# Weights applied in the expert stage: what a routed row carries, and who copies it

## The reference, cut to what matters

```python
xn = _layernorm(x)                        # x: (4, 1024, 256)
s = attention(xn)                         # 16 heads of 16, causal, with decay, then @ o_w.T + o_b
probs = softmax(xn @ gate_w)              # 8 experts
gate_score, gate_idx = top_k(probs, 2)
gate_score = gate_score / sum(gate_score)
combine = einsum('tk,tke->te', gate_score, onehot(gate_idx)) * alpha[None, :]
h = gelu(einsum('th,ehi->eti', xn, fc1_w) + fc1_b[:, None, :])
y = einsum('eti,eih->eth', h, fc2_w) + fc2_b[:, None, :]
g = silu(einsum('eth,te->th', y, combine))
out = x + s * g
```

## Time and profile before

| | us |
|---|---|
| median of 3 runs (703.76 to 708.72) | 706.3 |
| the profiled execution | 707.9 |
| its span, first to last instruction | 706.1 |
| TensorE busy | 681.8 (97%) |
| VectorE busy | 534.2 (76%) |
| ScalarE busy | 483.9 (69%) |
| GpSimd busy | 240.1 (34%) |
| mean granted TensorE clock | 0.980 |

### The profile page before, as it was taken

The page is one execution under the profiler, slowest core; times in us unless marked ns, Lnnn a source line. Parts: engine busy times, 40 slices in busy tenths (PEclk is TensorE's granted clock), DMA queues, the critical chain, the costliest instruction groups (busy, mean ns, idle before and its releaser), DMA issues.

```text
span 706.1 us, 16193 instructions
## 1 busy us (share of the span) xinstructions
PE 681.8 (97%) x5370; PEld 453.1 (64%) x5370; DVE 534.2 (76%) x1146; ACT 483.9 (69%) x994; POOL 240.1 (34%) x336
## 2 busy tenths in 40 slices
PE   7998999999999999999999999999999999999985
PEld 4886676455555556555555555554379999999764
DVE  6566887999999999999999999996234554444298
ACT  3553344577787877788787778878776666666374
POOL 4261211233023433333343332300035857575300
PEclk9999999899999999999999999999999999999998
DMA  6999786123445564555556456510189686855396
GB/s 209 283 302 369 250 268 206 36 76 80 106 150 134 137 184 138 146 158 169 132 141 174 147 135 160 157 41 19 47 191 282 243 227 194 240 177 176 123 396 248
DMA packets 74802, 124.46 MB, mean 176 GB/s; under 512 B 13832, under 2 KB 44296, under 8 KB 74600
## 3 DMA queue, kind: packets, MB, share of 16 engines
q1 hardware_dynamic: 65104, 95.26, 46.6%
q0 software_dynamic: 9616, 28.17, 12.4%
HBM read 72.64 MB, written 49.72 MB: 173 GB/s over the span
## 4 chain that ended last, share of the span: by engine, by line
PE 82%; DVE 9%; DMA 3%; ACT 2%; issue 2%; POOL 0%; SPq 0%; POOLq 0%; DVEq 0%; ACTq 0%
PE ps L1607 20%; PE ps L1591 14%; PE ps L1538 13%; PE ps L1695 9%; PE ps L1717 9%; PE ps L1527 6%; PE ps L1490 5%; DVE mxa L1132 3%; PE ps L1500 3%; PE ps L1678 2%; DMA q_parts<-arena 2%; ACT arena L993 1%; DVE x_room L1445 1%; DVE arena L1440 1%; DVE arena L1430 1%
## 5 line engine op out<-in xcount | busy, mean ns | idle before, releaser
L1132 DVE TENSOR_REDUCE mxa<-ps 128x1 f32<-128x512 f32 (+3 forms) x608 | 358.3, 655 | 34.8 <-PE ps L1527 21.2
L993 ACT ACTIVATE arena<-ps 128x512 f32<-128x512 f32 x576 | 302.8, 605 | 76.1 <-PE ps L1591 38.6
L1591 PE MATMUL ps<-aug 59*128 59x512 f32 (+3 forms) x768 | 216.4, 403 | 0.7 <-ACT arena L993 0.5
L1538 PE MATMUL ps<-aug 57*128 57x512 f32 (+3 forms) x768 | 212.5, 402 | 3.4 <-DVE mxa L1132 1.9
L1591 PEld LDWEIGHTS ps<-aug 59*128 59x128 f32 x768 | 112.5, 188 | 78.9 <-ACT arena L993 69.2
L1607 PE MATMUL ps<-arena,v_q 128*32 128x512 f32 (+3 forms) x1536 | 156.6, 503 | 1.0 <-ACT arena L993 1.0
L1538 PEld LDWEIGHTS ps<-aug 57*128 57x128 f32 x768 | 109.9, 188 | 41.6 <-DVE mxa L1132 25.2
L886 POOL DMA_INDIRECT xs_dram<-arena,slot x64 | 62.8, 981 | 81.9 <-ACT arena L993 78.5
L913 POOL DMA_INDIRECT y_dram<-arena,y_row_of x71 | 69.6, 981 | 47.0 <-DVE y_row_of L1369 38.6
L1527 PE MATMUL ps<-key_mask,key_rows 64*128 64x128 bf16 (+2 forms) x352 | 77.4, 254 | 0.0
L1695 PE MATMUL ps<-arena 128*128 128x128 f32 x568 | 75.2, 275 | 0.0
(11 more groups left out here) (150 smaller groups left out, 642.0 us busy)
## 6 DMA issues: line engine op xcount, KB each, us to landing
aug<-k_parts SPq DMA_DIRECT2D x96, 128.0 KB
aug<-q_parts SPq DMA_DIRECT2D x96, 128.0 KB
arena<-xs_dram SPq DMA_DIRECT2D x71, 128.5 KB
k_parts<-arena SPq DMA_DIRECT2D x16, 512.0 KB, 4.7
q_parts<-arena SPq DMA_DIRECT2D x16, 512.0 KB, 4.5
arena<-y_dram SPq DMA_DIRECT2D x16, 512.0 KB, 7.7
xn_dram<-arena SPq DMA_DIRECT2D x8, 512.0 KB, 5.6
a_dram<-arena SPq DMA_DIRECT2D x128, 32.0 KB
```

The source lines that it names most:

```text
L993: nc.scalar.activation(prob_slot(q, i), score_bank(q, i), ACT.Exp).then_inc(exp_done, 1)
L1132: nc.vector.tensor_reduce(dst, src, AX.X, ALU.max).then_inc(piece_used, 1)
L1538: ins = nc.tensor.matmul(banks[:, at_ * width:(at_ + 1) * width], k_aug[n][rows, hp, ib * P:(ib + 1) * P], q_aug[n][rows, hp, lo:lo + widt ...
L1591: ins = nc.tensor.matmul(out_[:, col0:col0 + hi - lo], q_aug[n][rows, h // SIDES_OF_ARRAY, jb * P:(jb + 1) * P], k_aug[n][rows, h // SIDES ...
```

## The change

A routed row is 258 words: row number, weight, 256 values. `scatter` copies the weight next to the number with a second small copy. In the expert stage `take_row` moves from VectorE to GpSimd and copies both words; three of these copies come ahead of GpSimd's loop, the others inside it, three tiles ahead of the store. VectorE, after the bias, multiplies the tile with its rows' weights in a second instruction; for this it waits for its own addition (`y_biased`) and for `row_taken`. TensorE waits for `y_biased` where it waited for `y_out`. `y_evacuate` takes the expert number from the register that `h_evacuate` read. In the last stage ScalarE's scaling is gone, and VectorE adds the two choices with one instruction for the pair. `row_and_weight` lies in the room of `logits`.

```diff
@@ -12,7 +12,8 @@
 
 P = 128
 B, T, D = 4, 1024, 256
-W = D + 1
+LEAD = 2
+W = D + LEAD
 H, HD = 16, 16
 E = 8
 KT = D // P
@@ -225,16 +226,6 @@
 
 def is_last(q):
     return isinstance(q, int) and q == NQ - 1
-
-
-def in_turn(ahead, what):
-
-    for m in range(AHEAD_OF_PRODUCT):
-        ahead(m)
-    for m in range(NT // 2):
-        what(m)
-        if m + AHEAD_OF_PRODUCT < NT // 2:
-            ahead(m + AHEAD_OF_PRODUCT)
 
 
 def attention_moe_kernel(nc, x, wqT, wkT, wvT, woT, qb, kb, vb, ob, gate, w1, b1, w2, b2, alpha,
@@ -295,14 +286,14 @@
         weight = sb("weight", [P, NT, 2])
         slot = sb("slot", [P, NT, 2], i32)
         tile_expert = sb("tile_expert", [P, SLOTS], i32)
-        y_row_of = sb("y_row_of", [P, SLOTS], i32)
+        row_and_weight = logits[:, :, :].rearrange("p t e -> p (t e)")[:, 0:LEAD * SLOTS].bitcast(i32).rearrange("p (n r) -> p n r", r=LEAD)
         y_row = sb("y_row", [P, NT, 2], i32)
         blank = sb("blank", [P, W])
-        zeros = blank[:, 1:W]
+        zeros = blank[:, LEAD:W]
         pad_slot = sb("pad_slot", [P, E], i32)
         spare_f = sb("spare_f", [P, E, 2])
         spare = sb("spare", [P, E, 2], i32)
-        ARENA = 16 * 1024 + CH
+        ARENA = 16 * 1024 + LEAD * CH
         arena = sb("arena", [P, ARENA])
         at = [0]
 
@@ -359,7 +350,7 @@
         b1_sb = cut(E * D).rearrange("p (e n) -> p e n", e=E)
         b2_sb = cut(E * D).rearrange("p (e n) -> p e n", e=E)
         at[0] = 0
-        xg = [x_move[:, j, 1:W] for j in range(CH)]
+        xg = [x_move[:, j, LEAD:W] for j in range(CH)]
         at[0] = 0
         xgT = [cut(D) for _ in range(CH)]
         w1_now = [cut(KT * D).rearrange("p (k n) -> p k n", k=KT) for _ in range(2)]
@@ -459,10 +450,10 @@
         xg_in = [sem(f"xg_in{n}") for n in range(CH)]
         t1_done = sem("t1_done"); xgT_out = sem("xgT_out"); l1_done = sem("l1_done"); h_out = sem("h_out")
         g_done = sem("g_done"); w1_ready = sem("w1_ready"); l2_done = sem("l2_done")
-        y_out = sem("y_out"); y_stored = [sem(f"y_stored{n}") for n in range(STEP)]
+        y_biased = sem("y_biased"); y_out = sem("y_out"); y_stored = [sem(f"y_stored{n}") for n in range(STEP)]
         x_all_in = sem("x_all_in"); a_in = [sem(f"a_in{b}") for b in range(B)]
         ya_in = [sem(f"ya_in{n}") for n in range(DEEP_Y)]
-        vb_turned = sem("vb_turned"); vb_out = sem("vb_out"); vb_done = sem("vb_done"); ob_step = sem("ob_step"); ob_split = sem("ob_split"); s_proj = sem("s_proj"); y_scaled = sem("y_scaled")
+        vb_turned = sem("vb_turned"); vb_out = sem("vb_out"); vb_done = sem("vb_done"); ob_step = sem("ob_step"); ob_split = sem("ob_split"); s_proj = sem("s_proj");
         gsum_done = sem("gsum_done"); silu_done = sem("silu_done"); sg_done = sem("sg_done")
         fin_done = sem("fin_done"); stored = sem("stored")
 
@@ -488,7 +479,8 @@
             return bass.AP(ap.tensor, ap.offset, [list(ap.ap[0]), [0, n]] + [list(x) for x in ap.ap[1:]])
 
         def many_zeros(n):
-            return bass.AP(zeros.tensor, zeros.offset, [list(zeros.ap[0]), [0, n], [1, D]])
+            first = blank[:, 1:W]
+            return bass.AP(first.tensor, first.offset, [list(first.ap[0]), [0, n], [1, W - 1]])
 
         best, first, second, gap, gexp, where, norm, low = col
 
@@ -724,7 +716,7 @@
 
         @block.gpsimd
         def _(pool):
-            nc.gpsimd.memset(zeros, 0.0).then_inc(zeros_set, 1)
+            nc.gpsimd.memset(blank[:, 1:W], 0.0).then_inc(zeros_set, 1)
             for n in range(AUG):
                 nc.gpsimd.memset(v_q[n][:, :, :, HD:2 * HD], 1.0).then_inc(ones_set, 1)
 
@@ -880,7 +872,9 @@
                 pool.wait_ge(scattered, 16 * (2 * first_tile + k * count))
                 nc.gpsimd.tensor_copy(x_move[:, 0:count, 0:1].bitcast(i32),
                                       y_row[:, first_tile:first_tile + count, k:k + 1]).then_inc(rows_ready, 1)
-                pool.wait_ge(rows_ready, 2 * r + k + 2)
+                nc.gpsimd.tensor_copy(x_move[:, 0:count, 1:2], weight[:, first_tile:first_tile + count, k:k + 1]
+                                      ).then_inc(rows_ready, 1)
+                pool.wait_ge(rows_ready, 2 * (2 * r + k) + 3)
                 for s in range(count):
                     pool.wait_ge(exp_done, NU * q + BETWEEN_BATCHES[k][s] + SCORE_BANKS + 1)
                     nc.gpsimd.indirect_dma_start(
@@ -895,7 +889,7 @@
                     pool.wait_ge(scattered, 16 * 2 * MOVES[r])
                 if q < FIRST_TAIL:
                     first_tile, count = MOVES[r], MOVES[r + 1] - MOVES[r]
-                    pool.dma_start(x_move[:, 0:count, 1:W], xn_t[:, first_tile:first_tile + count, :]).then_inc(x_moved, 16)
+                    pool.dma_start(x_move[:, 0:count, LEAD:W], xn_t[:, first_tile:first_tile + count, :]).then_inc(x_moved, 16)
                 next_v(q, q % AUG)
                 if PADS_FROM <= q < PADS_FROM + E:
                     clear_pads(q - PADS_FROM, q)
@@ -905,14 +899,22 @@
             for n in range(A_PIECES):
                 normalise(0, n)
 
+            def take_row(n):
+                pool.wait_ge(xg_in[n % CH], 16 * (n // CH) + 16)
+                nc.gpsimd.tensor_copy(row_and_weight[:, n, :], x_move[:, n % CH, 0:LEAD].bitcast(i32)).then_inc(row_taken, 1)
+
+            for n in range(CH - 1):
+                take_row(n)
             for n in range(SLOTS):
                 if n in NORMALISE_BESIDE:
                     normalise(*NORMALISE_BESIDE[n])
+                if n + CH - 1 < SLOTS:
+                    take_row(n + CH - 1)
                 pool.wait_ge(row_taken, n + 1)
-                pool.wait_ge(y_out, n + 3)
+                pool.wait_ge(y_out, n + 1)
                 nc.gpsimd.indirect_dma_start(
                     out=y_dram, in_=ysb[n % STEP], in_offset=None,
-                    out_offset=bass.IndirectOffsetOnAxis(ap=y_row_of[:, n:n + 1], axis=0)).then_inc(y_stored[n % STEP], 16)
+                    out_offset=bass.IndirectOffsetOnAxis(ap=row_and_weight[:, n, 0:1], axis=0)).then_inc(y_stored[n % STEP], 16)
 
 
         @block.scalar
@@ -1032,28 +1034,19 @@
 
             nc.scalar.activation(std[:, :], veps[:, :], ACT.Silu)
 
-            def scale_first(m):
-                j = m % DEEP
-                act.wait_ge(ya_in[m % DEEP_Y], 16 * (m // DEEP_Y) + 16)
-                if m >= DEEP:
-                    act.wait_ge(sg_done, m - DEEP + 1)
-                for i in range(2):
-                    ins = nc.scalar.activation(gsum[j][:, i * D:(i + 1) * D], ya[m % DEEP_Y][:, i, 0, :], ACT.Identity,
-                                               scale=weight[:, 2 * m + i, 0:1])
-                ins.then_inc(y_scaled, 1)
-
             def silu(m):
                 act.wait_ge(gsum_done, m + 1)
                 nc.scalar.activation(gsum[m % DEEP], gsum[m % DEEP], ACT.Silu).then_inc(silu_done, 1)
 
-            in_turn(scale_first, silu)
+            for m in range(NT // 2):
+                silu(m)
 
 
         @block.vector
         def _(dve):
             dve.sem_inc(piece_used, PIECE_BANKS)
             dve.sem_inc(h_out, 2)
-            dve.sem_inc(y_out, 2)
+            dve.sem_inc(y_biased, 2)
 
             def statistics(i, b, c):
                 if i == 1:
@@ -1364,13 +1357,10 @@
                 x_evacuate_first(n)
             evacuate(NQ - 1, 1)
 
-            def take_row(n, j):
-                dve.wait_ge(xg_in[j % CH], 16 * (n // CH) + 16)
-                nc.vector.tensor_copy(y_row_of[:, bass.ds(n, 1)], x_move[:, j % CH, 0:1].bitcast(i32)).then_inc(row_taken, 1)
-
+            expert_of = {}
 
             def h_evacuate(n, j):
-                e = dve.value_load(tile_expert[0:1, bass.ds(n, 1)], min_val=0, max_val=E - 1)
+                e = expert_of[n] = dve.value_load(tile_expert[0:1, bass.ds(n, 1)], min_val=0, max_val=E - 1)
                 dve.wait_ge(l1_done, n + 1)
                 nc.vector.tensor_tensor(hid[j % CH], bank(2 + j % 2)[:, 0:D], b1_sb[:, e, :], ALU.add).then_inc(h_out, 1)
 
@@ -1408,28 +1398,31 @@
                 if n == TURN_BIAS + 2:
                     dve.wait_ge(vb_turned, 1)
                     nc.vector.tensor_copy(vb_wide, bank(4)[:, 0:D]).then_inc(vb_out, 1)
-                e = dve.value_load(tile_expert[0:1, bass.ds(n, 1)], min_val=0, max_val=E - 1)
+                e = expert_of.pop(n)
                 dve.wait_ge(l2_done, n + 1)
                 if n >= STEP:
                     dve.wait_ge(y_stored[j % STEP], 16 * (n // STEP))
-                nc.vector.tensor_tensor(ysb[j % STEP], bank(6 + j % 2)[:, 0:D], b2_sb[:, e, :], ALU.add).then_inc(y_out, 1)
+                nc.vector.tensor_tensor(ysb[j % STEP], bank(6 + j % 2)[:, 0:D], b2_sb[:, e, :], ALU.add).then_inc(y_biased, 1)
+                dve.wait_ge(y_biased, n + 3)
+                dve.wait_ge(row_taken, n + 1)
+                nc.vector.tensor_scalar(ysb[j % STEP], ysb[j % STEP], row_and_weight[:, n, 1:2].bitcast(fp32), None,
```

(18 more changed lines are left out.)

## The result

The changed kernel takes 729.4 us (median of 4 runs, 725.4 to 731.1) against 705.0 (4 runs, 703.4 to 708.7) for the kernel before on the same chip: a ratio of 1.0312, 95% interval 1.0273 to 1.0351. The forecast of 716.2 and the range to 724 were too low; the sign was right. The profiled execution took 730.6 us with a span of 728.7, 22.6 more than the 706.1 of before.

What follows compares the result with a forecast made beforehand. TensorE was taken to bound the expert stage, VectorE the last. Terms 8.5 + 2.0 + 3.0 + 0.5 - 4.1 = +9.9 us on a profiled 707.9 gave 717.8, less 1.6 for that run: 716.2 us, range 710 to 724.

Steps and rivals of the forecast that it cites:

- Part 1: Expert stage start: row copies behind GpSimd's normalisation of batch 0 delay tile 4's fetch; TensorE stalls 8.5 us.
- Part 2: Behind that stall: TensorE restarts at the 1.2 GHz clock level, losing 2.0 us.
- Part 3: Steady expert tile: the fetch leaves 3.5 us after the transpose, has 4.4 to land against 2.8 taken; hidden.
- Part 4: 24 expert tiles with a normalisation: GpSimd's round becomes 2.17 us, fetches leave later, some beside 1 MB loads; 3.0 us lost.
- If the cover is thin: Caveat on the steady tile's fetch cover: inverse loads, also 128 KB and sent in bursts, landed in 5.0 us median.
- Part 5: Last stage: last store 0.46 us later, +0.5; VectorE's round falls from 1.99 to 1.80 us, -4.1.
- GpSimd blocked by the multiply: Rival, expert stage: each multiply holds GpSimd up by 0.17 to 0.29 us, adding 4 to 7; 722 us, chance 0.12.
- DMA-bound last stage: Rival: DMA sets the last stage's pace, its end moves by 2 us or less; 719 us, chance 0.12.
- Inverse sums sooner: Rival, expert stage start: inverse sums land 4 us earlier, so the stall is 4.5 us; 711 us, chance 0.09.

Runs made afterwards that it cites:

- e8: Changed kernel with four row copies ahead of GpSimd's first normalisation pieces and 21 of the 24 looped pieces left out; ratio 1.0153 to the kernel before.
- e3: Kernel before with VectorE's row copy two tiles ahead instead of three, so each fetch leaves one tile later; ratio 1.0135.
- e4: Changed kernel with four row copies ahead of GpSimd's first normalisation pieces and the 24 inverse-sum loads of batches 1 to 3 left out; ratio 1.0054.
- e9: Kernel before with only the change's last stage, the weights applied nowhere; ratio 0.9931.
- e7: Changed kernel with the copy of both words back on VectorE, behind the multiply, four tiles ahead; ratio 1.0003 to the kernel before.
- e11: Changed kernel with the copy of both words on VectorE, between bias addition and multiply; ratio 1.0009 to the kernel before.

## Why the prediction was wrong

**Part 1, right.** TensorE stood 9.1 us for 8.5, by the chain forecast. The landing was a little longer (3.1 for 2.8), and GpSimd began its pieces 0.7 us later than before, counted from TensorE's first transpose (5.9 for 5.2).

**Part 2, right in kind**: granted clock 0.50, 1.2 GHz, for about two tiles behind the stall; loss 1.6 us for 2.0. It was counted for that stall alone; two waits of the steady part brought it back, for 2.9 us more.

**Part 3, right in its times, wrong in its conclusion.** The fetch leaves 3.43 us after the transpose and has 4.48 to land. "Hidden, with 1.0 to 1.8 to spare" came from one landing of a lone load. A lone fetch lands even sooner, in 2.0 to 2.3 us. But many aren't alone: of the 62 fetches from tile 9 on, 18 took more than 4.48 us.

**Part 4, the step that failed.** It gave 3.0 us to "tiles with a normalisation" and to fetches beside 1 MB loads. Measured: 27.1 - 9.1 - 1.6 = 16.4 us. Its mechanism (the copy slips behind the piece, and the fetch leaves later still) is in the trace: GpSimd's rounds there are 2.1 us, and most fetches of tiles 19 to 28, 38 to 47 and 57 to 65 leave up to 4.9 us after the transpose. Most of them land in 1.9 to 3.1 us, and there it costs nothing. Where it may have counted is at tile 19 (left after 4.11 us, 2.1 of wait, and 1.5 behind it) and at tiles 47 and 48; e8 has no loss at tiles 19 and 20, but e3, with GpSimd's queue untouched, has 2.8 at tile 19. The main cost is where other loads share the engines: the 24 inverse-sum loads alone account for about 1% (e4), some 7 us. "If the cover is thin" was written beside the 5.0 us of the earlier trace rows, and then only a part of 3.0 us, for fetches beside the 1 MB loads too, put into the sum: 5.0 is above the 4.4 available in every tile that meets the inverse-sum loads, and there the fetches took up to 8.9. A late tile also makes its successor's fetch late, because this leaves only behind the bias addition and the copy. e3 shows the size of it in the kernel before: 9.8 us. How the 16.4 divide between late leaving, slipping behind the pieces and longer landings stays open.

**Part 5, right in the round, off by 1.3 us in the sum.** The rounds are 1.80; -2.3 in place of -3.6, mostly since VectorE now meets the DMA in the first round (0.93 us). e9, with the last store at its old time, shows -3.7 to -4.0.

**The rivals.** GpSimd blocked by the multiply: by 0.08 us a piece at most; VectorE is held more. DMA-bound last stage: in its first round only. Inverse sums sooner: no, GpSimd was released at 522.18, 1.4 earlier, in a stage that began 2.2 earlier. None of them had the cause; the 1.0 to 1.8 us "to spare" should itself have been a rival, priced by the landing times of loads in company.

## What to carry over

When a change moves the issue of a prefetch, compare the time it then has with the landing times of the busiest stretch, not of a lone load: windows with a DMA share near 1 in the kernel before are where cover is being spent unseen. A row copy that frees a buffer is best put where the load is released early and nothing waits for the copy's own input; whatever stands ahead of it in that queue, once or in every tile, is paid by the fetch. And a stage's gain is best measured alone first: here 0.7% was real, and the stage that had to pay for it gave back several times that.

## What was not expected of the hardware

VectorE's multiply by a per-partition scalar (128x256 fp32 in SBUF) takes 0.35 us alone, and up to 0.98 when a GpSimd elementwise instruction, or an issue of an indirect DMA begun some 0.3 us before, is under way: it ends 0.15 to 0.23 us after GpSimd's does. The copy of two words is held in the same way (0.69 us beside a piece in e7, in place of 0.18); the bias addition, with one operand in PSUM, kept its 0.42 us beside both. After TensorE had been idle for 2.14 us, the granted clock was 0.54 to 0.61. A fetch of 129 KB lands in 2.0 us alone and in up to 9.7 (tile 50 of e11) beside other loads; in the changed kernel up to 8.9, with the DMA share at 1.04 to 1.09 and the rate at 180 to 265 GB/s, where the last stage moves 383 (720 to 721 us) at 1.09, and 408 at 1.07 in the earlier trace rows.
